# Half of each row normalisation moved from VectorE to ScalarE, with the result stored from the normalised rows' tile and a newly written step order

## The chip, the cores and the metric

The kernel runs on one core of a Trainium2 chip. The metric is device time in microseconds (us): from the start to the end of one execution. Five engines run their own instruction queues beside each other: TensorE (PE, matmuls and transposes; PEld is its loading of stationary operands), VectorE (DVE), ScalarE (ACT), GpSimd (POOL) and SyncE (SP, which issues nearly all DMAs here). An engine works through its queue strictly in the order in which the program writes it, and a semaphore wait at its head holds everything behind it.

## The reference, cut to what matters

The input `x` has 128 batches of 64 tokens of width 128, all fp32. `cond` gives each batch a vector and `ctx` each batch 64 context tokens. Four layers are applied one after the other:

```python
def _ln(x):                       # in every layer, before each projection
    mu = jnp.mean(x, axis=-1, keepdims=True); var = jnp.var(x, axis=-1, keepdims=True)
    return (x - mu) * jax.lax.rsqrt(var + EPS)
# layer 0 and layer 2 (16 heads of width 8, MLP of width 512)
xm = _ln(x) * (1.0 + sc_sa) + sh_sa              # sc, sh, g from silu(cond) @ W
x  = x + g_sa * (self_attention(xm @ W_qkv) @ W_proj)
x  = x + cross_attention(_ln(x) @ W_q, context) @ W_proj
xm = _ln(x) * (1.0 + sc_ff) + sh_ff
x  = x + g_ff * (gelu(xm @ W1 + b1) @ W2 + b2)
# layer 1: modulated cross attention; layer 3: router over 3 experts, and a gate
x = x + g * (routed @ out_w + out_b)
```

A group of four batches needs eight layer norms of `x` on its way through the four layers.

## The kernel before, in words

Four batches (256 tokens) make a group, 32 groups in all. A group's rows lie in a tile of 128 partitions x 2 x 128: two row blocks, t=0 and t=1. Six streams, s=0 to 5, each with its own set of tiles, work on six groups at once; a stream takes group s, then s+6, and so on. A group is 91 steps (`GROUP_STEPS`): load, stats, normal, context, cols, q, k, v, tops, lows, scores, values, out, and so on to l3_out and store. Each step may put instructions on several engines.

**What sets the order.** `SEQUENCE` is a string of 2930 characters. A digit means "the next step of that stream", an `f` means "the next of the 18 set-up steps" (`FOLDS`: modulations, gates, products of weights). `interleave()` turns it into `ORDER`, and every engine writes its instructions by walking through `ORDER`. So the one string fixes the order on all engines. It consists of a head of 243 steps, a piece of 546 steps (six groups) that stands four times in a row, and an end of 503 steps. `HALVES` says for each of the 320 attention score sets which half of PSUM it takes.

**A layer norm** goes over four engines: `stats` (lines 1097 to 1104) lets VectorE take means and variances; POOL adds eps and takes the power -0.5 (lines 696, 698, tile `rstd`); `normal` (line 1109) lets VectorE compute `(x - mean) * rstd` for t=0 and t=1 into `n_rows`; `cols` (line 740) lets TensorE transpose `n_rows`, after which VectorE modulates it, or ScalarE moves it, into `nT`. Between two stream steps of one stream stand steps of the other streams. POOL also prepares `lifted`, the residual plus bias (lines 708 and 711), and waits there for `gates`.

**The end of a group** (lines 1218 to 1220 and 651 to 656): VectorE writes the result over `x_rows`; SP stores `x_rows`, waits until the store has landed, and only then loads the next group into `x_rows`.

**The start.** SP issues conditions, small tables, the whole 1 MB of modulation weights, then rows and contexts of streams 0, 2 and 1 between further weights (lines 601 to 611). It waits for the gates' rows, stores them, waits, loads gates of four streams, and after that issues the other pieces of weights (line 598). TensorE's first `turn` step (line 786) waits for all the weights.

The code that the change touches, and what calls it:

## Time and profile before

| | |
|---|---|
| three timed runs | 1860.48, 1850.87, 1860.58 us; median 1860.48 |
| the profiled execution, its own time | 1857.61 us |
| its span, first to last instruction | 1855.6 us |
| around the span | 2.0 us |
| TensorE's granted clock over the span | 0.996 |
| PE busy, matmul instructions | 1758.5 us, 38181 |
| DVE busy | 1638.5 us |
| ACT busy | 1382.8 us |
| POOL busy | 643.6 us |

The profile names an instruction by its line in the kernel, its engine and the tiles it writes and reads (`out<-in`, buffer numbers left out, and `half` is PSUM). Each fp32 matmul shows as two records. Busy time of an engine is the union of its instructions' durations. "Idle before" is the engine's gap before an instruction, and the releaser is the instruction, on another engine, whose end let it go; "issue" is a gap that the profile puts down to nothing. A window's busy time over its length shows how close an engine is to filling it.

### The profile page before, as it was taken

What the parts mean: (1) busy time and instruction counts of PE and PEld (TensorE: products, weight loads), DVE (VectorE), ACT (ScalarE), POOL (GpSimd) and SP (SyncE); (2) the same over time, 40 slices, a digit from 0 to 9 for tenths busy, and PEclk for the clock granted to TensorE, in tenths of its full rate; (3) what the DMA queues carried; (4) which work ended last, traced back from release to release, by engine and by line L of the source; (5) the groups of instructions that cost most, each with busy time, mean ns of one, the idle gap of its engine ahead of it and who ended that gap; (6) DMA issues with size and microseconds to landing.
All of it is one profiled execution on the core that took longest, in us unless ns stands there. A gap on an engine that the chain in (4) does not pass through costs nothing.

```text
span 1855.6 us, 88109 instructions
## 1 busy us (share of the span) xinstructions
PE 1758.5 (95%) x38181; PEld 1505.4 (81%) x38181; DVE 1638.5 (88%) x4238; ACT 1382.8 (75%) x3341; POOL 643.6 (35%) x1145
## 2 busy tenths in 40 slices
PE   5988999999999999999999999999999999999898
PEld 4767788888788888888888888888888788887788
DVE  5889889999899999998999999899999989998874
ACT  2655777787787877777887787787777777777696
POOL 4222333343342343333233334233333333432341
PEclk9999999999999999999999999999999999999999
DMA  6000000001000000000000000000000000000000
GB/s 220 3 20 4 17 23 23 9 17 29 17 23 23 18 12 20 23 23 23 23 9 18 23 23 23 23 11 15 23 23 23 23 14 17 20 13 7 8 6 15
DMA packets 57693, 42.09 MB, mean 23 GB/s; under 512 B 13536, under 2 KB 56160, under 8 KB 57056
## 3 DMA queue, kind: packets, MB, share of 16 engines
q1 hardware_dynamic: 57312, 36.46, 6.7%
q8 instruction: 306, 5.01, 1.1%
q14 instruction: 75, 0.61, 0.1%
HBM read 31.99 MB, written 4.46 MB: 20 GB/s over the span
## 4 chain that ended last, share of the span: by engine, by line
PE 75%; DVE 13%; ACT 6%; issue 4%; DMA 0%; SPq 0%; POOL 0%; DVEq 0%; POOLq 0%
PE half L990 9%; PE half L888 8%; PE half L866 8%; PE half L892 7%; PE half L907 7%; PE half L935 5%; PE half L925 5%; DVE top L1136 4%; PE half L999 4%; PE half L740 4%; PE half L853 4%; PE half L918 3%; PE half L842 3%; PE half L838 3%; ACT pT L1335 2%
## 5 line engine op out<-in xcount | busy, mean ns | idle before, releaser
L1300 ACT ACTIVATE pT<-half 128x512 f32<-128x512 f32 x640 | 328.0, 610 | 103.2 <-PE half L892 102.2
L696 POOL TENSOR_TENSOR shifted<-moments,eps 128x2 f32<-128x2 f32 x256 | 50.6, 198 | 1010.7 <-DVE moments L1103 1010.7
L1136 DVE TENSOR_REDUCE top<-half 128x32 f32<-128x2048 f32 x160 | 365.0, 2281 | 30.7 <-PE half L866 29.3
L888 PE MATMUL half<-o_rows,of_keys 32*128 32x128 f32 x5120 | 274.4, 281 | 6.2 <-ACT o_rows L1229 2.9
L892 PE MATMUL half<-q_heads,k_heads 32*128 32x128 f32 x5120 | 262.2, 270 | 1.4 <-issue 1.3
L1335 ACT ACTIVATE pT<-half,mod 128x64 f32<-128x64 f32 x896 | 196.2, 332 | 54.3 <-PE half L990 53.2
L888 PEld LDWEIGHTS half<-o_rows,of_keys 32*128 32x128 f32 x5120 | 207.1, 186 | 29.1 <-issue 14.6
L892 PEld LDWEIGHTS half<-q_heads,k_heads 32*128 32x128 f32 x5120 | 209.1, 187 | 1.9 <-issue 1.9
L1276 ACT ACTIVATE k_heads<-half,key_bias,own_head_sb 128x256 f32<-128x256 f32 x320 | 163.4, 571 | 51.0 <-PE half L842 49.5
L866 PE MATMUL half<-k_heads,q_heads 32*128 32x128 f32 x5120 | 189.0, 281 | 9.6 <-issue 5.2
L1109 DVE TENSOR_SCALAR n_rows<-x_rows,moments,rstd 128x128 f32<-128x128 f32 x512 | 188.9, 415 | 6.8 <-POOL rstd L698 6.0
L698 POOL TENSOR_TENSOR rstd<-shifted,minus_halves 128x2 f32<-128x2 f32 x256 | 185.2, 723 | 20.1
L866 PEld LDWEIGHTS half<-k_heads,q_heads 32*128 32x128 f32 x5120 | 160.6, 186 | 37.4 <-issue 21.3
L907 PE MATMUL half<-pT,v_cols 128*32 128x64 f32 x10240 | 177.8, 221 | 10.3 <-issue 5.1
L907 PEld LDWEIGHTS half<-pT,v_cols 128*32 128x32 f32 x10240 | 153.7, 110 | 41.1 <-issue 32.4
L1128 DVE TENSOR_SCALAR q_heads<-half,b_sb,own_head_sb 128x256 f32<-128x256 f32 x320 | 156.5, 532 | 12.3 <-PE half L838 11.8
L1284 ACT ACTIVATE v_cols<-half 64x256 f32<-64x256 f32 x320 | 122.6, 383 | 24.6 <-PE half L853 22.4
L990 PE MATMUL half<-nT,w_sb 128*128 128x256 f32 x448 | 138.1, 390 | 0.1
L925 PE MATMUL half<-nT,w_sb 128*128 128x256 f32 x512 | 135.9, 394 | 1.0 <-DVE nT L1116 0.5
L1141 DVE STREAM_TRANSPOSE q_heads<-half 128x512 f32<-128x512 f32 x160 | 113.3, 708 | 26.3 <-PE half L907 23.6
L1305 ACT ACTIVATE pT<-half,b_sb 128x256 f32<-128x256 f32 x256 | 106.0, 471 | 38.5 <-PE half L925 37.3
L990 PE MATMUL half<-pT,w_sb 128*128 128x256 f32 x448 | 133.9, 380 | 0.6 <-issue 0.6
(148 smaller groups left out, 3755.2 us busy)
## 6 DMA issues: line engine op xcount, KB each, us to landing
gates<-gate_store SPq DMA_DIRECT2D x128, 128.0 KB, 3.1
x_rows<-x SPq DMA_DIRECT2D x32, 128.0 KB, 2.3
c_rows<-context SPq DMA_DIRECT2D x32, 128.0 KB, 2.4
out<-x_rows SPq DMA_DIRECT2D x32, 128.0 KB, 1.8
w_sb<-weights SPq DMA_DIRECT2D x1, 1856.0 KB, 10.5
pT<-weights SPq DMA_DIRECT2D x1, 1024.0 KB, 5.1
w_sb<-weights SPq DMA_DIRECT2D x2, 512.0 KB, 5.2
logit_bias<-logit_store SPq DMA_DIRECT2D x64, 1.5 KB, 3.5
```

Source lines behind the costliest of these rows:

```text
L698: nc.gpsimd.tensor_tensor(rstd[s][:, :], shifted[s][:, :], minus_halves[:, 0, :], ALU.pow).then_inc(rstd_in[s], 1)
L866: mm = nc.tensor.matmul(halves[HALF_OF[n]][:, g, tb * D:(tb + 1) * D], q_heads[s][part, tb, :, :], k_heads[s][part, tb, :, :], start=True, ...
L888: nc.tensor.matmul(halves[HALF_OF[n]][:, g, tb * D:(tb + 1) * D], of_keys[part, 2 * tb:2 * tb + 2, :], low[s][part, :], start=True, stop=F ...
L892: mm = nc.tensor.matmul(halves[HALF_OF[n]][:, g, tb * D:(tb + 1) * D], k_heads[s][part, tb, :, :], q_heads[s][part, tb, :, :], start=False ...
L907: mm = nc.tensor.matmul(dst[QUAD * g:QUAD * (g + 1), tb, :, lo, :], v_cols[s][:, at:at + QUAD], pT[s][:, g, tb, lo, :].rearrange("p (h q) ...
L925: mm = nc.tensor.matmul(dst[:, c * TOK:(c + 1) * TOK], w(layer["w1"], 0, 2 * half + c), nT[s][:, :, :], start=True, stop=True)
L990: mm = nc.tensor.matmul(dst[:, r * TOK:(r + 1) * TOK], weight, src[:, :, :], start=c == 0, stop=c == 1)
L1109: m = nc.vector.tensor_scalar(n_rows[s][:, t, :], x_rows[s][:, t, :], moments[s][:, t, 0:1], rstd[s][:, t:t + 1], ALU.subtract, ALU.mult)
L1136: nc.vector.tensor_reduce(top[s][:, :].rearrange("p (g c) -> p g c", c=32)[:, :, 0:2 * GROUP], halves[HALF_OF[n]][:, :, :].rearrange("p g ...
L1276: m = nc.scalar.activation(k_heads[s][:, :, pair, :], bank4(src), ACT.Identity, scale=own_head[:, pair:pair + 1], bias=key_bias[:, n_att, ...
L1300: nc.scalar.activation(turn_cols[s][:, g, :], halves[HALF_OF[n]][:, g, :], ACT.Exp, scale=ATT_SCALE).then_inc(scores_read, 1)
L1335: m = nc.scalar.activation(dst, src[:, at], ACT.Silu, bias=mod[s][:, k, tb:tb + 1])
```

## The change

1. **normal.** VectorE normalises only t=0. POOL computes one more value, `minus = -mean * rstd` for t=1 (128x1), and ScalarE normalises t=1 as `Identity(rstd * x + minus)`. TensorE's transposes wait for both (`rows_normed` counts to 2).
2. **End of a group.** VectorE writes the result into `added`, which is the same tile as `n_rows`. SP stores from there and issues the next group's `x` at once. The wait for the store moves to VectorE, before the next group's `stats` (and for all streams to SP's end).
3. **Start.** Of the modulation weights the 768 columns of layer 0 come first; the other 1280 columns follow after layer 0's own weights, with a semaphore of their own (`later_mods_in`) that `gates` waits for. All remaining weights and the fourth stream's rows are issued ahead of the wait for the gates' rows. The copy of the first modulations to a stream moves from `load` to the first `cols`.
4. **Order.** `SEQUENCE` and `HALVES` are new strings, of the same lengths (2930 and 320), again a head of 243 steps, 546 steps four times, and an end of 503. Tiles that set-up borrows from streams now go by the order in which streams start or score.

```diff
-    "ff02410210002300f202f0222f110f320313f203201f0100f301132f010410f31024203f202111f310023f1014f2041f3001"
+    "f023101200f0f11100f02104312f10102f31303120f23021f00023f04312f01420f11201f40310f32300f22104f22031f020"
...
-                load_weights(W_LOADS[0], 0, W_LOADS[0][3], mod_weights_in)
-                load_rows(0)
+                load_weights(W_LOADS[0], 0, MOD_L0_COLS, mod_weights_in)
+                load_rows(BY_START[0])
                 load_weights(W_LOADS[1], 0, L0_COLS, l0_weights_in)
-                load_rows(2)
+                load_weights(W_LOADS[0], MOD_L0_COLS, W_LOADS[0][3] - MOD_L0_COLS, later_mods_in)
+                load_rows(BY_START[1])
...
                 load_weights(W_LOADS[1], L0_COLS, W_LOADS[1][3] - L0_COLS, weights_in)
+                for load in W_LOADS[2:]:
+                    load_weights(load, 0, load[3], weights_in)
+                load_rows(BY_START[3])
 
                 sp.wait_ge(v_emptied, used_by(FOLD_AT["gates", None], FOR_VECTOR))
                 sp.dma_start(gate_store, gate_rows[0:B, :]).then_inc(gates_stored, 16)
-                load_rows(3)
                 sp.wait_ge(gates_stored, 16)
...
-                        sp.dma_start(rows_of(out, s, r), x_rows[s][:, :, :]).then_inc(stored[s], 16)
-                        sp.wait_ge(stored[s], 16 * (r + 1))
+                        sp.dma_start(rows_of(out, s, r), added[s][:, :, :]).then_inc(stored[s], 16)
                         if r + 1 < ROUNDS[s]:
                             sp.dma_start(x_rows[s][:, :, :], rows_of(x, s, r + 1)).then_inc(x_in[s], 16)
...
+                        count.next(rstd_in[s])
+                        nc.gpsimd.tensor_scalar(minus[s][:, :], moments[s][:, 1, 0:1], -1.0, rstd[s][:, 1:2], ALU.mult, ALU.mult).then_inc(minus_in[s], 1)
...
                     if kind == "cols":
-                        count.next(rows_normed[s])
+                        count.next(rows_normed[s], 2)
...
                     if kind == "gates":
+                        pe.wait_ge(later_mods_in, 16)
...
                     if kind == "stats":
                         dve.wait_ge(*x_changed(n))
+                        if residual_before(n)[0] is None and round_of(n):
+                            dve.wait_ge(stored[s], 16 * round_of(n))
...
                     if kind == "normal":
                         count.next(rstd_in[s])
-                        for t in range(2):
-                            m = nc.vector.tensor_scalar(n_rows[s][:, t, :], x_rows[s][:, t, :], moments[s][:, t, 0:1], rstd[s][:, t:t + 1],
-                                                        ALU.subtract, ALU.mult)
-                        m.then_inc(rows_normed[s], 1)
+                        nc.vector.tensor_scalar(n_rows[s][:, 0, :], x_rows[s][:, 0, :], moments[s][:, 0, 0:1], rstd[s][:, 0:1],
+                                                ALU.subtract, ALU.mult).then_inc(rows_normed[s], 1)
...
-                        nc.vector.scalar_tensor_tensor(out=x_rows[s][:, :, :], in0=added[s][:, :, :], scalar=0.5, in1=x_rows[s][:, :, :],
+                        nc.vector.scalar_tensor_tensor(out=added[s][:, :, :], in0=added[s][:, :, :], scalar=0.5, in1=x_rows[s][:, :, :],
                                                        op0=ALU.mult, op1=ALU.add).then_inc(x_added[s], 1)
...
+                    if kind == "normal":
+                        count.next(minus_in[s])
+                        nc.scalar.activation(n_rows[s][:, 1, :], x_rows[s][:, 1, :], ACT.Identity, scale=rstd[s][:, 1:2],
+                                             bias=minus[s][:, :]).then_inc(rows_normed[s], 1)
```

What the new order makes of the engines' queues is shown at three places. First TensorE in the start, before, from the end of the first exp scores on. `half0<-ident_sb,w_sb` (L786) is the first `turn` step, `top2` the second stream's maxima, and `o_rows2,of_keys` begins the second stream's scores:

```order
L740 MATMUL half0<-ident_sb,n_rows1 128x128 x2
L740 MATMUL half0<-ident_sb,c_rows3 128x128 x2
L786 MATMUL half0<-ident_sb,w_sb 128x128
L786 MATMUL half0<-ident_sb,pT4 128x128 x2
L786 MATMUL half0<-ident_sb,w_sb 128x128
L877 MATMUL half0<-ident_sb,top2 128x128
L907 MATMUL half0<-pT0,v_cols0 32x2x32 x32
L740 MATMUL half0<-ident_sb,n_rows3 128x128 x2
L888 MATMUL half1<-o_rows2,of_keys 128x128 x4
```

The same place now; the second stream to start is stream 1, and L753, L775, L800, L891, L902 and L921 are the former L740, L762, L786, L877, L888 and L907:

```order
L753 MATMUL half0<-ident_sb,n_rows2 128x128 x2
L775 MATMUL half0<-pT4,pT5 128x128 x4
L891 MATMUL half0<-ident_sb,top1 128x128
L753 MATMUL half0<-ident_sb,c_rows3 128x128 x2
L921 MATMUL half0<-pT0,v_cols0 32x2x32 x32
L753 MATMUL half0<-ident_sb,n_rows3 128x128 x2
L902 MATMUL half1<-o_rows1,of_keys 128x128 x4
```

The `turn` step that waits for all weights has moved from before the first values (`pT0,v_cols0`) and the second scores to behind them.

Second, VectorE at its first instructions of the loop, before: modulations, their copies and the statistics of three streams.

```order
L1050 TENSOR_SCALAR mods<-half,b_sb 128x128 x4
L1029 COPY mod<-mods 128x16 x4
L1100 BN_STATS stats<-x_rows 128x6 x2
L1103 BN_AGGR moments<-stats 128x2 x2
L1100 BN_STATS stats<-x_rows 128x6 x2
L1103 BN_AGGR moments<-stats 128x2 x2
L1100 BN_STATS stats<-x_rows 128x6 x2
L1103 BN_AGGR moments<-stats 128x2 x2
L1109 TENSOR_SCALAR n_rows<-x_rows,moments,rstd 128x128 x2
```

And now:

```order
L1113 BN_STATS stats<-x_rows 128x6 x2
L1116 BN_AGGR moments<-stats 128x2 x2
L1113 BN_STATS stats<-x_rows 128x6 x2
L1116 BN_AGGR moments<-stats 128x2 x2
L1113 BN_STATS stats<-x_rows 128x6 x2
L1116 BN_AGGR moments<-stats 128x2 x2
L1121 TENSOR_SCALAR n_rows<-x_rows,moments,rstd 128x128
L1103 BN_STATS c_stats<-c_rows 128x6 x2
L1105 BN_AGGR c_moments<-c_stats 128x2 x2
L1064 TENSOR_SCALAR mods<-half,b_sb 128x128 x4
L1043 COPY mod<-mods 128x16
```

The statistics of three streams still stand ahead of the first normalisation; the modulations have moved behind it.

Third, ScalarE's queue in the repeated piece, as it is now (before, its queue held no `n_rows`). L1319 is the exp of the scores, L1295, L1303 and L1243 move keys, values and other tiles out of PSUM:

```order
L1319 ACT_TABLE_LOAD
L1319 ACTIVATE pT1<-half1 128x512 x4
L1360 ACTIVATE kvT3<-kvT3 128x256
L1295 ACTIVATE k_heads5<-half0,key_bias,own_head_sb 128x4x64 x2
L1303 ACTIVATE v_cols5<-half0 64x32x8 x2
L1279 ACTIVATE n_rows5<-x_rows5,minus5,rstd5 128x128
L1279 ACTIVATE n_rows4<-x_rows4,minus4,rstd4 128x128
L1295 ACTIVATE k_heads2<-half0,key_bias,own_head_sb 128x4x64 x2
```

The normalisation of t=1 stands between moves out of PSUM, and whatever follows it on ScalarE waits if POOL's `minus` is late.

## Rows read from the trace of the kernel before

**Rows 1.** The page: busy times of the engines, and the chain that ended last, by engine.

```profile
PE 1758.5 (95%) x38181; PEld 1505.4 (81%) x38181; DVE 1638.5 (88%) x4238; ACT 1382.8 (75%) x3341; POOL 643.6 (35%) x1145
...
PE 75%; DVE 13%; ACT 6%; issue 4%; DMA 0%; SPq 0%; POOL 0%; DVEq 0%; POOLq 0%
```

**Rows 2.** Windows: length, then busy us (instructions) of each engine; granted clock; DMA share; GB/s.

```profile
0.00:165.00 165.00, 127.23 (x2852) 106.17 (x2856) 125.67 (x320) 76.61 (x175) 48.94 (x108) 0.97 0.22 69
165.00:1492.00 1327.00, 1290.45 (x28394) 1105.59 (x28390) 1208.60 (x3136) 1031.63 (x2475) 478.47 (x842) 1.00 0.07 20
655.32:986.02 330.70, 324.21 (x7141) 278.15 (x7141) 304.09 (x788) 260.50 (x625) 119.95 (x211) 1.00 0.07 20
1492.00:1800.00 308.00, 290.85 (x6541) 247.92 (x6536) 276.14 (x691) 233.00 (x540) 102.39 (x176) 1.00 0.04 12
```

**Rows 3.** Chain that ended last, whole span, 200 longest pieces: start, us, what.

```profile
324.06 3.65 PE half L990 x16
...
1318.91 3.65 PE half L990 x16
```

**Rows 4.** Waits of PE in one period: releaser, us in total, times, longest.

```profile
PE half L740 <- ACT pT L1335: 1.2, 1, 1.2
PE half L877 <- DVE n_rows L1022: 0.8, 1, 0.8
PE half L907 <- issue: 0.7, 1, 0.7
...
PE half L877 <- DVE top L1136: 0.3, 1, 0.3
```

**Rows 5.** Chain that ended last, 0 to 60 us: start, us, what.

```profile
7.02 6.76 DMA x_rows<-x
...
33.53 6.91 issue
...
44.22 0.46 PE half L888 x8
```

**Rows 6.** Timeline of SP's DMA issues, 0 to 60 us: start, us, what.

```profile
21.30 0.34 SPq L615 DMA_DIRECT2D gate_store<-pT  x1
...
23.38 5.99 SPq L582 DMA_DIRECT2D gates<-gate_store  x8
...
35.04 0.43 SPq L598 DMA_DIRECT2D pT<-weights  x1
```

**Rows 7.** Timeline of PE, 0 to 60 us: start, us, what, idle before.

```profile
41.67 1.94 PE L907 MATMUL half<-pT,v_cols 128*32 128x64 f32 x64
...
53.10 1.10 PE L907 MATMUL half<-pT,v_cols 128*32 128x64 f32 x64
```

**Rows 8.** Timeline of DVE, 0 to 60 us.

```profile
9.94 1.13 DVE L1050 TENSOR_SCALAR mods<-half,b_sb 128x128 f32<-128x128 f32 x4 [3.44 <-PE half L762]
...
14.49 0.57 DVE L1109 TENSOR_SCALAR n_rows<-x_rows,moments,rstd 128x128 f32<-128x128 f32 x2
```

**Rows 9.** Timeline of POOL, 0 to 75 us.

```profile
28.19 0.73 POOL L708 TENSOR_TENSOR lifted<-gates,row_sb 128x256 f32<-128x256 f32 x1 [10.27 <-DMA gates<-gate_store]
```

**Rows 10.** Groups of instructions by shape: count, busy us, mean ns, idle before.

```profile
L1109 DVE TENSOR_SCALAR n_rows<-x_rows,moments,rstd 128x128 f32<-128x128 f32 x512 | 188.9, 415 | 6.8 <-POOL rstd L698 6.0
...
L1259 ACT ACTIVATE nT<-c_rows,c_minus,c_rstd 128x128 f32<-128x128 f32 x128 | 56.2, 496 | 0.1
...
L693 POOL TENSOR_SCALAR c_minus<-c_minus 128x4 f32<-128x4 f32 x32 | 7.4, 232 | 2.9
```

**Rows 11.** Who waited for the normalised rows (L1109): us, times.

```profile
  PEld half L740: 14.1, 14
```

**Rows 12.** SP's transfers of x_rows, who waited for one, and the page's store and load.

```profile
  DVE stats L1100: 0.5, 1
...
x_rows<-x SPq DMA_DIRECT2D x32, 128.0 KB, 2.3
out<-x_rows SPq DMA_DIRECT2D x32, 128.0 KB, 1.8
```

More of the change, by code:

```diff
@@ L215 @@
-    "0000011110001110001111111111100000000111110000001111110000011111100001111011111111110000110000110000"
-    "00001000001001111100"
+    "0011110011110011111100110011000011100011111111111000001110000011111110000011111100001111100011100011"
+    "1111111110000011100000111111100000111111000011111000111000111111111110000011100000111111100000111111"
+    "0000111110001110001111111111100000111000001111111000001111110000111110001001110000111110000011111001"
+    "11110000110011111111"
 )
@@ L273, in first_scores @@
     return min(n for n, (kind, _, t) in enumerate(ORDER) if kind == "scores" and t == s)
+BY_SCORES = sorted(range(STREAMS), key=first_scores)
+BY_START = sorted(range(STREAMS), key=lambda s: min(n for n, (kind, _, t) in enumerate(ORDER) if kind == "stats" and t == s))
+assert max(FOLD_AT.values()) < first_scores(BY_SCORES[4])
 def next_step(n):
@@ L426, in build @@
         shifted, rstd = each("shifted", [D, 2]), each("rstd", [D, 2])
+        minus = each("minus", [D, 1])
         c_shifted, c_rstd, c_minus = each("c_shifted", [D, 2, 2]), each("c_rstd", [D, 2, 2]), each("c_minus", [D, 2, 2])
@@ L470, in build @@
         routed = n_rows
-        early = {MOD_ONLY: turn_cols[5].rearrange("p n c -> p (n c)"), SET_UP_ONLY: turn_cols[4].rearrange("p n c -> p (n c)")}
-        turned = turn_cols[5][:, 0:3, :].rearrange("p n (m c) -> p (n m) c", c=D)
-        gate_rows, gate_bias = turn_cols[3][:, 3, :], gates[5][:, :, :, :].rearrange("p t n c -> p (t n) c")
-        cond_rows, cond_silu, logit_rows = turn_cols[4][0:B, 3, 0:D], turn_cols[4][:, 3, D:D + B], turn_cols[4][:, 3, 2 * D:2 * D + EXPERTS]
+        early = {MOD_ONLY: turn_cols[BY_SCORES[5]].rearrange("p n c -> p (n c)"), SET_UP_ONLY: turn_cols[BY_SCORES[4]].rearrange("p n c -> p (n c)")}
+        turned = turn_cols[BY_SCORES[5]][:, 0:3, :].rearrange("p n (m c) -> p (n m) c", c=D)
+        gate_rows, gate_bias = turn_cols[BY_SCORES[3]][:, 3, :], gates[BY_START[5]][:, :, :, :].rearrange("p t n c -> p (t n) c")
+        spare = turn_cols[BY_SCORES[4]][:, 3, :]
+        cond_rows, cond_silu, logit_rows = spare[0:B, 0:D], spare[:, D:D + B], spare[:, 2 * D:2 * D + EXPERTS]
         logit_store = nc.dram_tensor("logit_store", (B, EXPERTS), F32, kind="Internal").ap()
@@ L482, in build @@
         small_in = first_sem
-        mod_weights_in, l0_weights_in, weights_in, rows_in, gate_bias_in = (sem(name) for name in (
-            "mod_weights_in", "l0_weights_in", "weights_in", "rows_in", "gate_bias_in"))
+        mod_weights_in, later_mods_in, l0_weights_in, weights_in, rows_in, gate_bias_in = (sem(name) for name in (
+            "mod_weights_in", "later_mods_in", "l0_weights_in", "weights_in", "rows_in", "gate_bias_in"))
         consts_made, key_bias_made = sem("consts_made"), sem("key_bias_made")
@@ L504, in build @@
         o_turned = sem("o_turned")
+        minus_in = [sem(f"minus_in{s}") for s in range(STREAMS)]
         p3_done, p3_normed = [sem(f"p3_done{s}") for s in range(STREAMS)], [sem(f"p3_normed{s}") for s in range(STREAMS)]
@@ L652, in _ @@
                         sp.wait_ge(*x_changed(n))
-                        sp.dma_start(rows_of(out, s, r), x_rows[s][:, :, :]).then_inc(stored[s], 16)
-                        sp.wait_ge(stored[s], 16 * (r + 1))
+                        sp.dma_start(rows_of(out, s, r), added[s][:, :, :]).then_inc(stored[s], 16)
                         if r + 1 < ROUNDS[s]:
                             sp.dma_start(x_rows[s][:, :, :], rows_of(x, s, r + 1)).then_inc(x_in[s], 16)
+                for s in range(STREAMS):
+                    sp.wait_ge(stored[s], 16 * ROUNDS[s])
             @block.gpsimd
```

79 lines of the change are left out of this document (38 added, 41 removed).

## The prediction

> **What bounds the kernel now.** I read the page's busy times and its chain first. TensorE is busy for 1758.5 of 1855.6 us (95%), VectorE for 88%, ScalarE for 75%, and three quarters of the chain that ended last are TensorE's [rows 1]. So TensorE is the bound, and the change removes no matmul: all that can be won is its idle time, 1855.6 - 1758.5 = 97 us, and what the order lets it do faster. A table by windows shows where those 97 us lie [rows 2]. I cut it at the repetitions of the step order, which show in the trace as a period: the same long block of L990 stands at 324.06 us and, three repetitions later, at 1318.91 us, so 331.6 us each [rows 3]. Until 165 us TensorE is idle for 165.0 - 127.2 = 38 us. In the repeated part, 165 to 1492 us, it is idle for 1327.0 - 1290.5 = 36.5 us, 2.8%, and in one period for 330.7 - 324.2 = 6.5 us. From 1492 to 1800 us it is idle for 17 us, while VectorE is busy for 276 of 308 us (90%). In the last 56 us it is idle for 6 us, in a drain that the change leaves alone.
>
> Then I read who ends the idle time. In the second of those periods VectorE ended five waits of TensorE worth 2.0 us (0.8 us the longest, 0.3 us the last), ScalarE four worth 2.1 us (1.2 us the longest), and "issue" three worth 1.6 us [rows 4]. No wait stands out, and VectorE ended about a third. In the start one does: 6.91 us from 33.53 us on, in the chain, put down to "issue" [rows 5]. It is TensorE at the first `turn` step. The profile names no releaser, but the step waits for all weights, and the last of them were issued at 35.04 us, because SP had waited for the gates' rows (stored at 21.30 us) and then issued eight gate loads (23.38 to 29.37 us) ahead of them [rows 6].
>
> **The change part by part.** I make the sum against the profiled execution: 1857.6 us, 2.0 us more than its span. The median of the three runs is 1860.5 us, 2.9 us above it; the number at the end is on the median's scale.
>
> *The start.* All weights are now issued ahead of the wait for the gates' rows, and the `turn` step stands behind the first values and the second scores. The 6.9 us go. Of two equal blocks of values, the one behind the gap took 1.94 us and the next 1.10 us [rows 7], so another 0.8 us goes with it. The first window's granted clock is 0.97 and the later ones' 1.00 [rows 2]. The page "TensorE: Matmul & The Clock Gate" of the Trainium skill, part 1, says that an idle TensorE falls from 2.4 to 1.2 GHz and needs sustained work to come back. By that rule a gap of this length costs more than itself, which the two blocks agree with; without the rule the term would be 6.9 us alone.
>
> Against this stand two delays. VectorE still takes three streams' statistics before its first normalisation, and the third stream's x landed at 7.02 + 6.76 = 13.78 us [rows 5]. The queue ahead of it holds the same bytes in another order (768 + 1280 columns for 2048), so splitting the modulation weights wins nothing there. But the modulations (four instructions, 1.13 us [rows 8]) now stand between that normalisation and its modulation: +1 us. And the gate rows' store now queues behind twelve more weight loads and a stream's rows, some 2.3 MB. Before, the weights took from 29.4 us, when SP began to issue them, until TensorE's release at 40.4 us: 11 us. Now their issue begins some 12 us before the store's 21.3 us. I take the store as 0 to 5 us late. POOL stood waiting for these gates until 28.19 us [rows 9], and now `lifted` of two streams and then the fourth stream's `rstd` stand behind that wait. Late by 5 us, it would release them at 33 us, and the second stream's scores would follow some 4 us later. Before, they began at 44.22 us [rows 5], so this is covered up to about 7 us. Start: -6.9 - 0.8 + 1.0 = -6.7, say -7 us; bounds -11 (the second scores come as early as the queues allow) and +3 (the gates take all of it).
>
> *Half the normalisation.* VectorE loses 256 of 512 instructions of 188.9/512 = 0.37 us busy each: 94 us. ScalarE gains 256. The nearest row is its normalisation of the context, same shape and source, 56.2/128 = 0.44 us each [rows 10]: 113 us. POOL gains 256 instructions near `c_minus` at 0.23 us: 59 us. By period, with 48 of them, VectorE goes from 304 to 286 us, ScalarE from 260 to 282 us, POOL from 120 to 131 us, all against TensorE's 324 [rows 2]. No engine overtakes TensorE. The Trainium skill's "ScalarE: Activation LUTs", under its rules for kernel authors, says adds and multiplies belong on VectorE, not ScalarE. The rows agree in price, 0.44 against 0.37 us, and by the rule the work of both grows by 18 us. It would decide only if ScalarE were full; that is the third rival.
>
> VectorE with 6% less to do hands its results over earlier. I take the third of TensorE's idle time that VectorE ends: 36.5/3 = 12 us in the repeated part and 17/3 = 6 us between 1492 and 1800 us, of which I take 5, since the end's order must also empty six streams. Bounds: nothing, if TensorE's other releasers are just behind, and all of the 36.5 and 17 us.
>
> *The longer path of a norm.* Before: `rstd`, then VectorE's pair, 0.57 us where nothing disturbs it [rows 8]. Now: `rstd`, 0.23 us on POOL, then 0.50 us (the mean) on ScalarE [rows 10]: +0.16 us, which I round up to 0.24 us for the gap between two dependent instructions on POOL, a choice of mine. That is 256 x 0.24 = 61 us if nothing covered it. TensorE's weight loads waited for normalised rows 14 times [rows 11]; only there is it uncovered: 14 x 0.24 = 3 us. Bounds 3 and 30 us (half uncovered). Behind a late `minus` on ScalarE stand moves of keys and values out of PSUM, and TensorE waits for those.
>
> *Store and load.* SP no longer holds 26 times for a store of 1.8 us before it loads x (2.3 us). VectorE waited 0.5 us for x in the whole trace, once [rows 12], so the gain is 0. The new wait on VectorE, for a store issued ahead of that load and landing sooner, is 0 too; if it were late, statistics and everything behind them on VectorE would wait. The later copy of the modulations is the same instruction in another place: 0.
>
> Sum: 1857.6 - 7 - 12 - 5 + 3 = 1836.6 us, and 2.9 us more on the median's scale: 1839.5, so 1840 us.
>
> **The rivals.**
>
> 1. *Only the start.* TensorE's waits in the repeated part are short and spread over three kinds of releaser [rows 4]. If taking VectorE out of a wait only uncovers ScalarE's, now busier, the period stays at 331 us. For it: no wait of over 1.2 us in a period. Against it: the chain runs through VectorE for 13% and ScalarE for 6% [rows 1]. Then -7 and -2 at the end: 1851.5, so 1852 us.
> 2. *The new order is better than VectorE's relief alone.* With the order rewritten the idle time in the repeated part could halve and the end lose 10 us: -10 - 18 - 10 + 3 = -35, so 1826 us. For it: some of the 324 us busy per period may be blocks stretched by late operands. Against: the piece repeated has the same 546 steps.
> 3. *ScalarE becomes the late engine: slower.* Its queue holds blocks of four exps and table loads. A t=1 half that falls behind one is late for TensorE's transposes, where VectorE's pair was in time, and a late `minus` holds moves out of PSUM. If half of the 256 norms expose 0.24 us, that is 31 us; less the start's 7 and a few of VectorE's relief it gives 1860.5 + 31 - 13 = 1878 us. It decides once ScalarE's queue runs more than about 0.3 us behind on most norms, and would show as a period above 335 us. Against it: ScalarE at 282 of 331 us keeps 15% of slack.
> 4. *The start does not do what it says.* The gate rows' store waits so long behind the weights that POOL's wait passes 35 us and TensorE stands idle for as long as before. With rival 1 that is 1859 us.
>
> **How the numbers follow.** Forecast, 1840 us: 0.47, own range 1828 to 1852. Rival 1, 1852 us: 0.26. Rival 2, 1826 us: 0.13. Rival 3, 1878 us: 0.10. Rival 4, 1859 us: 0.04. A change under about 0.5%, 9 us, can't be told from none here. Faster than 1851: 0.45 of the forecast, all of rival 2 and a third of rival 1, 0.66. Within 0.5%: the rest of these, and rival 4, 0.24. Slower than 1870: rival 3, 0.10. The range reaches from 1822, 4 us under rival 2, to 1862, past rivals 1 and 4, and leaves out rival 3 and a tail of rival 2.
>
> **What would show it.** Start: no gap of TensorE over 3 us between 30 and 45 us, the second scores at 33 to 38 us, POOL's wait for gates ending between 28 and 33 us. Repeated part: a period of 328 to 330 us, VectorE near 286 and ScalarE near 282 us in it, and less idle time before TensorE ended by VectorE. Norms: the ScalarE normalisation near 0.44 us busy each, POOL's `minus` near 0.23 us. End: less than 14 us idle of TensorE in the 300 us before the last 56. The prediction is wrong in its middle term if the period stays at 331 us, and wrong in sign if it exceeds 335 us with ScalarE as TensorE's main releaser.

## The result and the profile after

The changed kernel took 1833.6 us in the median of four runs (1830.3 to 1836.0), the kernel before 1860.0 us in four runs beside it (1850.9 to 1860.6): a ratio of 0.9877, 95% interval 0.9855 to 0.9898, 1.2% faster (the two medians alone, divided, give 0.986). I had forecast 1840 us, range 1822 to 1862. The profiled execution took 1832.7 us with a span of 1830.8 us, 24.8 us less than the span before; the sum had promised 21.

Busy times of the engines and the chain that ended last, of the changed kernel's page (against [rows 1]):

```profile
PE 1751.3 (96%) x38181; PEld 1503.1 (82%) x38181; DVE 1554.5 (85%) x3982; ACT 1484.3 (81%) x3598; POOL 717.2 (39%) x1401
...
PE 83%; DVE 8%; ACT 5%; issue 3%; DMA 1%; SPq 1%; DVEq 0%
```

VectorE lost 84 us, ScalarE gained 102, POOL 74. TensorE's own busy time fell by 7 us, and it now holds 83% of the chain instead of 75%. The same long block of `projected` matmuls, L1004 now, in the chain that ended last (start, us, what):

```profile
471.51 3.46 PE half L1004 x16
798.03 3.46 PE half L1004 x16
1128.62 3.46 PE half L1004 x16
1457.32 3.46 PE half L1004 x16
```

That is (1457.32 - 471.51) / 3 = 328.6 us a period, 3.0 less than the 331.6 of [rows 3]; four periods give 12 us. One by one they take 326.5, 330.6 and 328.7 us, against 331.3, 330.7 and 332.9 before. The windows, with the columns of [rows 2]; the second line is the longest of the three periods:

```profile
190.00:1500.00 1310.00, 1282.65 (x28420) 1104.88 (x28418) 1145.74 (x2934) 1119.50 (x2685) 528.91 (x1024) 1.00 0.07 20
798.03:1128.62 330.59, 323.25 (x7141) 278.29 (x7141) 288.07 (x739) 281.82 (x676) 133.50 (x258) 1.00 0.07 20
1500.00:1775.00 275.00, 262.57 (x5899) 222.54 (x5898) 234.59 (x590) 217.35 (x532) 108.44 (x209) 1.00 0.04 13
```

In a period VectorE is busy for 288 us (forecast 286) and ScalarE for 282 (forecast 282). All three periods in one window, first of the kernel before and then of the changed one:

```profile
324.06:1318.91 994.85, 972.97 (x21422) 834.51 (x21421) 910.36 (x2358) 781.48 (x1875) 358.37 (x631) 1.00 0.07 20
```

```profile
471.51:1457.32 985.81, 967.65 (x21422) 833.14 (x21421) 865.59 (x2221) 846.38 (x2027) 401.19 (x777) 1.00 0.08 20
```

For the same 21422 matmul records TensorE is busy 5.3 us less, and it is idle for 18.2 us instead of 21.9. So of the 3.0 us that a period lost, 1.8 are matmuls that took less time and only 1.2 are idle time. In these windows the view of waits gives VectorE 6.6 us of TensorE's idle time before (18 waits) and 4.6 now (8), ScalarE 6.6 (16) and 2.5 (8), and "issue" 6.7 (9) and 9.2 (15).

In the 275 us before the last 56, TensorE is idle for 12.4 us. The kernel before, cut the same way (1525 to 1800 us), was idle for 17.1:

```profile
1525.00:1800.00 275.00, 257.85 (x5870) 218.77 (x5869) 246.98 (x617) 206.28 (x479) 92.47 (x159) 1.00 0.05 14
```

The start on TensorE: the first normalised rows, the first scores, the first values, the second stream's scores and the first `turn` step (L800) of the changed kernel (start, us, what, idle before; against [rows 5, 7]):

```profile
15.98 0.69 PE L753 MATMUL half<-ident_sb,n_rows 128*128 128x128 f32 x2 [6.70 <-DVE n_rows L1121]
...
30.59 0.50 PE L902 MATMUL half<-o_rows,of_keys 32*128 32x128 f32 x8 [1.11 <-DVE mods L1064]
...
34.86 1.10 PE L921 MATMUL half<-pT,v_cols 128*32 128x64 f32 x64 [0.44 <-ACT pT L1319]
36.26 0.50 PE L902 MATMUL half<-o_rows,of_keys 32*128 32x128 f32 x8
...
39.23 0.27 PE L800 MATMUL half<-ident_sb,w_sb 128*128 128x128 f32 x1
```

No gap before the `turn` step, and the second scores begin at 36.3 instead of 44.2 us, 8 us earlier. The first block of values takes 1.10 us, where the one behind the gap took 1.94 [rows 7]. The window behind the gap, in the kernel before, shows a granted clock of 0.50:

```profile
40.44:43.70 3.26, 3.26 (x70) 2.76 (x71) 0.03 (x1) 0.77 (x2) 1.10 (x2) 0.50 0.59 139
```

In the changed kernel it is 1.00 in the block of values and in the second scores. POOL still waits for the gates, until 30.8 us (against [rows 9]):

```profile
30.78 0.73 POOL L721 TENSOR_TENSOR lifted<-gates,row_sb 128x256 f32<-128x256 f32 x1 [8.23 <-DMA gates<-gate_store]
```

And the three instructions of the split, by shape (count, busy us, mean ns, idle before; against [rows 10]):

```profile
L1279 ACT ACTIVATE n_rows<-x_rows,minus,rstd 128x128 f32<-128x128 f32 x256 | 127.4, 504 | 29.6 <-POOL minus L711 27.6
...
L1121 DVE TENSOR_SCALAR n_rows<-x_rows,moments,rstd 128x128 f32<-128x128 f32 x256 | 98.2, 390 | 12.3 <-POOL rstd L709 11.8
L711 POOL TENSOR_SCALAR minus<-moments,rstd 128x1 f32<-128x1 f32 x256 | 73.7, 288 | 26.2
```

By the group's row ScalarE's half costs 0.50 us of busy time, not 0.44, and POOL's `minus` 0.29, not 0.23.

So the start, the length of a period, the busy times in it and the end showed what I had forecast; where a period's 3.0 us come from did not. And that the places agree doesn't show that the parts of the change earn what I gave them, and the experiments say that they don't.

### The profile page after: what moved, and what is told of

Its sections match the earlier page's. It is cut to its first block, busy times and chain, and to the rows that moved or that the text cites. A ratio compares the mean times of both kernels' runs of the same rounds, so it can differ in the third digit from the quotient of the medians.

```text
span 1830.8 us, 88396 instructions
## 1 busy us (share of the span) xinstructions
PE 1751.3 (96%) x38181; PEld 1503.1 (82%) x38181; DVE 1554.5 (85%) x3982; ACT 1484.3 (81%) x3598; POOL 717.2 (39%) x1401
## 4 chain that ended last, share of the span: by engine, by line
PE 83%; DVE 8%; ACT 5%; issue 3%; DMA 1%; SPq 1%; DVEq 0%
PE half L1004 10%; PE half L902 8%; PE half L880 8%; PE half L921 8%; PE half L906 7%; PE half L939 6%; PE half L949 6%; PE half L1013 4%; PE half L753 4%; PE half L932 4%; PE half L867 4%; PE half L852 4%; PE half L856 3%; DVE top L1150 3%; ACT pT L1319 1%
## 5 line engine op out<-in xcount | busy, mean ns | idle before, releaser
L1319 ACT ACTIVATE pT<-half 128x512 f32<-128x512 f32 x640 | 330.0, 607 | 76.0 <-PE half L906 74.9
L902 PE MATMUL half<-o_rows,of_keys 32*128 32x128 f32 x5120 | 277.2, 282 | 7.8 <-issue 4.8
L902 PEld LDWEIGHTS half<-o_rows,of_keys 32*128 32x128 f32 x5120 | 208.5, 186 | 31.1 <-issue 18.7
L921 PE MATMUL half<-pT,v_cols 128*32 128x64 f32 x10240 | 177.7, 220 | 9.2 <-ACT pT L1319 4.6
L921 PEld LDWEIGHTS half<-pT,v_cols 128*32 128x32 f32 x10240 | 153.3, 110 | 38.7 <-issue 31.9
L1295 ACT ACTIVATE k_heads<-half,key_bias,own_head_sb 128x256 f32<-128x256 f32 x320 | 164.3, 573 | 24.3 <-PE half L856 22.7
L1279 ACT ACTIVATE n_rows<-x_rows,minus,rstd 128x128 f32<-128x128 f32 x256 | 127.4, 504 | 29.6 <-POOL minus L711 27.6
L1113 DVE BATCH_NORM_STATS2 stats<-x_rows 128x6 f32<-128x128 f32 x512 | 122.4, 281 | 21.5 <-DMA x_rows<-x 18.4
L1303 ACT ACTIVATE v_cols<-half 64x256 f32<-64x256 f32 x320 | 122.7, 383 | 20.6 <-PE half L867 17.6
L1004 PE MATMUL half<-nT,w_sb 128*128 128x256 f32 x448 | 137.1, 387 | 2.1 <-issue 2.1
L1004 PE MATMUL half<-pT,w_sb 128*128 128x256 f32 x448 | 133.2, 379 | 0.7 <-issue 0.7
L949 PE MATMUL half<-w_sb,pT 128*128 128x128 f32 x1024 | 127.5, 277 | 1.0 <-DVE top L1150 0.6
```

The source lines that it names most:

```text
L902: nc.tensor.matmul(halves[HALF_OF[n]][:, g, tb * D:(tb + 1) * D], of_keys[part, 2 * tb:2 * tb + 2, :], low[s][part, :], start=True, stop=F ...
L921: mm = nc.tensor.matmul(dst[QUAD * g:QUAD * (g + 1), tb, :, lo, :], v_cols[s][:, at:at + QUAD], pT[s][:, g, tb, lo, :].rearrange("p (h q) ...
L949: mm = nc.tensor.matmul(dst[:, t * D:(t + 1) * D], hidden[s][:, c, t * D:(t + 1) * D], w(arg["w2"], c), start=c == 0, stop=c == 3)
L1004: mm = nc.tensor.matmul(dst[:, r * TOK:(r + 1) * TOK], weight, src[:, :, :], start=c == 0, stop=c == 1)
L1295: m = nc.scalar.activation(k_heads[s][:, :, pair, :], bank4(src), ACT.Identity, scale=own_head[:, pair:pair + 1], bias=key_bias[:, n_att, ...
L1319: nc.scalar.activation(turn_cols[s][:, g, :], halves[HALF_OF[n]][:, g, :], ACT.Exp, scale=ATT_SCALE).then_inc(scores_read, 1)
```

## The experiments

Each ratio is against the kernel before, on the same chip, with a 95% interval; the kernel before had medians of 1856.6, 1852.4 and 1855.8 us in the three sets. Edits are against the changed kernel unless the text says "before".

### The split and the order, apart

**e1: the new order, both halves on VectorE.**

```diff
-                        count.next(rows_normed[s], 2)
+                        count.next(rows_normed[s])
...
-                        nc.vector.tensor_scalar(n_rows[s][:, 0, :], ...).then_inc(rows_normed[s], 1)
+                        for t in range(2):
+                            m = nc.vector.tensor_scalar(n_rows[s][:, t, :], ..., ALU.subtract, ALU.mult)
+                        m.then_inc(rows_normed[s], 1)
...
-                        nc.gpsimd.tensor_scalar(minus[s][:, :], ...)
-                        nc.scalar.activation(n_rows[s][:, 1, :], ...)
```

> The changed kernel with VectorE normalising both halves again, in the new order; POOL's minus and ScalarE's half are gone. Theory (VectorE's relief carries the repeated part and the end, 17 us of the 26 gained): 1848 to 1855 us, the period back to 331 us or more, VectorE near 304 us busy in it. Rival (the new order does it, whoever normalises): 1830 to 1838 us.

1.0006 (0.9993 to 1.0018): nothing. The new order, the new start and the new store, all three together but without the split, are worth nothing. Waits of TensorE in this kernel (releaser, us in total, times, longest):

```profile
PE half L751 <- DVE n_rows L1120: 18.1, 22, 6.9
```

The same line of the changed kernel:

```profile
PE half L753 <- DVE n_rows L1121: 9.5, 5, 6.7
PE half L753 <- ACT n_rows L1279: 1.7, 4, 0.8
```

With both halves on VectorE, TensorE waits for normalised rows 22 times instead of 9. The start's gain is there in e1 too (second scores at 35.3 us), and the repeated part gives it back: its block of L1011 returns after 335.2 and then 332.6 us.

The matmuls of e1 and of the changed kernel stand in the same order, so the two can be laid side by side. The block near the end of the repeated part and the one just before the drain, first in e1 and then in the changed kernel (chain that ended last; start, us, what):

```profile
1477.02 3.46 PE half L1002 x16
1800.74 3.46 PE half L1002 x16
```

```profile
1457.32 3.46 PE half L1004 x16
1774.60 3.46 PE half L1004 x16
```

e1 is 19.7 us behind at the first and 26.1 at the second, and 26.2 at the end of the span. In this order the split is worth 19.7 us up to the first block and 6.4 us from there to the second.

**e3: before, with the split alone, in the old order.** The edit is e1's, the other way round, on the kernel before.

```diff
+                        count.next(rstd_in[s])
+                        nc.gpsimd.tensor_scalar(minus[s][:, :], moments[s][:, 1, 0:1], -1.0, rstd[s][:, 1:2], ALU.mult, ALU.mult)...
...
-                        count.next(rows_normed[s])
+                        count.next(rows_normed[s], 2)
...
+                    if kind == "normal":
+                        count.next(minus_in[s])
+                        nc.scalar.activation(n_rows[s][:, 1, :], x_rows[s][:, 1, :], ACT.Identity, ...)
```

> The kernel before with only the normalisation split between VectorE and ScalarE, old order, old start, old end of a group. Theory: 12 us in the repeated part and 5 at the end, less 3 for the longer path: 1843 to 1850 us. Rival (ScalarE late in an order not made for it): 1860 to 1880 us.

1.0635 (1.0612 to 1.0657): 116 us slower. Busy times in the page of e3:

```profile
PE 1792.0 (91%) x38181; PEld 1522.8 (77%) x38181; DVE 1560.9 (79%) x3982; ACT 1486.8 (76%) x3597; POOL 714.2 (36%) x1401
```

VectorE's and ScalarE's work are those of the changed kernel within 7 us; neither is full (79 and 76%). The waits of TensorE, and of ScalarE, in e3:

```profile
PE half L744 <- ACT n_rows L1267: 55.8, 49, 3.1
PE half L744 <- DVE n_rows L1112: 5.0, 3, 4.7
...
ACT n_rows L1267 <- POOL minus L702: 63.5, 36, 8.2
```

One of the 49 in e3's chain that ended last (start, us, what):

```profile
700.43 1.28 ACT L1307
701.72 0.01 issue
701.73 4.03 ACT pT L1307 x8
705.75 0.37 ACT n_rows L1267
706.12 0.04 issue
706.16 0.44 PE half L744 x2
```

ScalarE's half stands behind a table load and eight exps, and the transposes come 3.14 us late. POOL's `minus` for this half had long been there (timelines of POOL and of PE):

```profile
696.42 0.27 POOL L702 TENSOR_SCALAR minus<-moments,rstd 128x1 f32<-128x1 f32 x1
```

```profile
706.16 0.44 PE L744 MATMUL half<-ident_sb,n_rows 128*128 128x128 f32 x2 [3.14 <-ACT n_rows L1267]
```

So it is in all 49 waits of the trace: `minus` was ready at least 1.2 us, in the median 4.3 us, before TensorE had come to the transposes, and the half itself takes 0.50. In 25 of them the instruction just ahead of the half on ScalarE is an exp, in 23 a move of values. A late `minus` counts only indirectly: in 6 of the 49 the unbroken row of ScalarE's work ahead of the half had begun when a `minus` arrived. Of the 110 us by which e3's span is longer, 76 are idle time of TensorE and 34 longer matmuls.

**e2: the changed kernel with the old order.** `SEQUENCE` and `HALVES` are the old strings, all else is new.

> The changed kernel's code with the strings of the order of before. Theory (relief and start work in any order, since ScalarE has room): 1838 to 1848 us. Rival (the order is what gains; ScalarE's half stands where nobody planned it): 1853 to 1865 us.

1.063 (1.0601 to 1.0659), the same as e3: both my expectations were wrong. Together e1 to e3 and the change itself make a table:

| | both halves on VectorE | t=1 on ScalarE |
|---|---|---|
| old order | 1 | 1.0635 (e3), 1.063 (e2, with the new start and store) |
| new order | 1.0006 (e1) | 0.9877 (the change) |

The parts don't add. The split costs 6.3% in the old order and wins 1.3% in the new one.

**e13: before with the split, and ScalarE's half still further back.** ScalarE's half is issued at the `cols` step instead of the `normal` step, behind what ScalarE does between the two.

```diff
-                    if kind == "normal":
+                    if kind == "cols":
                         count.next(minus_in[s])
                         nc.scalar.activation(n_rows[s][:, 1, :], ...)
```

> The kernel before with the split alone, and ScalarE's half written at the cols step instead of the normal step, so that minus is surely there and ScalarE holds nothing up, but the half starts later. If ScalarE's loss in the old order is its waiting for minus (63.5 us) with other work queued behind: ratio 1.00 to 1.03 instead of 1.06. If it is that the half comes too late for TensorE (55.8 us in 49 waits): 1.06 or more, with longer waits of TensorE for n_rows.

1.2427 (1.2387 to 1.2468). Waits in e13, and then its busy times:

```profile
PE half L744 <- ACT n_rows L1267: 345.9, 208, 3.4
...
ACT n_rows L1267 <- POOL minus L702: 3.5, 1, 3.5
```

```profile
PE 1895.0 (82%) x38181; PEld 1591.1 (69%) x38181; DVE 1562.9 (68%) x3982; ACT 1496.9 (65%) x3597; POOL 711.5 (31%) x1401
```

Between e3 and e13 only the half's place in ScalarE's queue differs, and the late norms go from 49 to 208; in the new order they are 4. ScalarE's wait for `minus` is gone in e13 (3.5 us), and it is the slowest of all. By itself that doesn't clear `minus` in e3, since the edit also makes the half later; the 49 waits above do. What makes the half late is its place in ScalarE's queue, against that of the transposes in TensorE's.

### The start

**e5: the changed kernel with the old SP order.**

```diff
-                load_weights(W_LOADS[0], 0, MOD_L0_COLS, mod_weights_in)
+                load_weights(W_LOADS[0], 0, W_LOADS[0][3], mod_weights_in)
...
-                for load in W_LOADS[2:]:
-                    load_weights(load, 0, load[3], weights_in)
...
                 sp.wait_ge(gates_stored, 16)
...
+                for load in W_LOADS[2:]:
+                    load_weights(load, 0, load[3], weights_in)
```

> The changed kernel with SP's start as before: modulation weights in one load, the other weights issued behind the gate loads. Theory (the turn step now stands behind the second scores, so the order alone hides most of the 6.9 us, but the weights land only near 40 us): 1833 to 1838 us, 0 to 4 us slower than the changed kernel. Rival (SP's order is what removed the gap): 1839 to 1843 us.

0.9878 (0.9865 to 0.9892), the ratio of the change itself. TensorE shows no gap at the `turn` step and the second scores begin at 35.4 us. The start's gain comes from the string, which puts that step behind the second scores; SP's order adds nothing to it. What it costs is late gates. In e5 POOL has the gates at 24.1 us:

```profile
24.11 0.73 POOL L720 TENSOR_TENSOR lifted<-gates,row_sb 128x256 f32<-128x256 f32 x1 [2.77 <-DMA gates<-gate_store]
```

In the changed kernel it has them 6.7 us later. There the gate rows' store was issued at 19.69 us and the gates' loads, which SP issues when it has landed, at 26.73; in e5 at 18.30 and 20.35. Those 6.7 us make no difference in time that can be told.

**e6: before, with only the weights and the fourth stream's rows ahead of the gates' wait.**

```diff
+                for load in W_LOADS[2:]:
+                    load_weights(load, 0, load[3], weights_in)
+                load_rows(3)
...
                 sp.wait_ge(gates_stored, 16)
...
-                for load in W_LOADS[2:]:
-                    load_weights(load, 0, load[3], weights_in)
```

> The kernel before with one edit: all weights and the fourth stream's rows issued ahead of the wait for the gates' rows. Theory (the gap at the turn step goes, the gates come a few us later): 6 to 8 us faster than before, 1849 to 1851 us. Rival (the later gates, which POOL waits for, take it back): within 2 us of before, 1855 to 1859 us.

0.998 (0.9968 to 0.9993), 3.7 us. The 6.9 us at the `turn` step are gone, but another wait stands just behind. TensorE's timeline in e6, the first values and the second scores:

```profile
38.30 1.79 PE L907 MATMUL half<-pT,v_cols 128*32 128x64 f32 x64 [3.83 <-DVE nT L1116]
...
40.65 0.81 PE L888 MATMUL half<-o_rows,of_keys 32*128 32x128 f32 x8
```

The chain that ended last names it (start, us, what):

```profile
25.98 2.88 DMA gates<-gate_store
...
29.03 0.74 POOL lifted L708
...
36.04 0.73 POOL rstd L698
36.77 0.03 issue
36.80 0.60 DVE n_rows L1109 x2
37.40 0.35 DVE half L1115
...
37.77 0.43 DVE nT L1116
```

POOL waits for the gates, does 7 us of other work that had queued behind them, then the `rstd` on which TensorE's next tile depends. Over half of the removed gap is given back there. The 3.7 us lie between my two expectations.

**e10: the changed kernel, with the first stream's statistics and normalisation ahead of the others'.** One line of `SEQUENCE`:

```diff
-    "f023101200f0f11100f02104312f..."
+    "f0231000f01f111200f02104312f..."
```

> The changed kernel, and in the first steps the first stream's statistics and normalisation come first, the second's statistics behind its modulation, the third's after that; TensorE's order is unchanged. In the changed kernel TensorE waited 6.7 us for the first normalised rows, until 15.98 us. Theory (the start is kept by the stream that waits): the first transposes at 9 to 10 us and 3 to 6 us off the time, ratio to before 0.984 to 0.986. Rival (the gate rows, which POOL waits for until 30.8 us, are the bound of the start): the ratio stays at 0.987 to 0.989.

0.9864 (0.9846 to 0.9882). The first normalised rows reach TensorE at 9.6 instead of 16.0 us, yet it then waits 4.22 us before the first scores for the modulations, and 1.36 us for ScalarE's half of normalised rows just ahead of the second stream's scores, which begin at 37.2 us. The interval holds the change's ratio: no difference that can be told.

**e11: e10, with the gates' rows stored ahead of the last weights and the fourth stream's rows.**

> The kernel of e10_stats_later, and SP issues the gate rows' store and then the last weights and the fourth stream's rows, before it waits for the store. Theory of the gates: POOL's wait ends by 27 us instead of 30.8, the second scores begin by 32 us, and another 2 to 4 us go: ratio 0.981 to 0.985. Rival: no more than e10_stats_later.

0.9868 (0.9854 to 0.9881). The store is issued at 14.3 instead of the 20.2 us of e10 and the gates' loads from 21.6 instead of 27.1 us on, but POOL has them only at 30.7 us, as before the edit (30.9 in e10). I had expected them earlier; the moved issue didn't bring the data sooner. The second scores begin at 36.2 us, behind a wait of 4.62 us for ScalarE's half. What the gates wait for, the weights in flight or something else, wasn't separated.

### The size of the smaller terms

**e4: store from `x_rows`, SP waits, then loads, as before the change.**

```diff
-                        sp.dma_start(rows_of(out, s, r), added[s][:, :, :]).then_inc(stored[s], 16)
+                        sp.dma_start(rows_of(out, s, r), x_rows[s][:, :, :]).then_inc(stored[s], 16)
+                        sp.wait_ge(stored[s], 16 * (r + 1))
```

> The changed kernel with the result written over x again, stored, waited for, and only then x loaded. Theory as predicted (early load worth nothing): 1831 to 1836 us. Rival (the new order puts the next group's statistics so close behind its load that VectorE waits 18 us for x already; 2 us more in each of 26 loads then cost TensorE some): 1840 to 1855 us.

0.9902 (0.9884 to 0.9921), 0.0025 or some 5 us more than the change, with intervals that overlap. VectorE waited for x for 23.0 us in e4. Who waited for a load of `x_rows`, in the changed kernel (against [rows 12]):

```profile
  DVE stats L1113: 18.4, 8
```

The old order left 0.5 us of such waits, this one 18.4, in which the early load can be worth something.

**e8: VectorE computes t=1 too, into a spare tile that nobody reads.** It waits for its own result.

```diff
+                        own_result(nc.vector.tensor_scalar(spare_rows[:, :], x_rows[s][:, 1, :], moments[s][:, 1, 0:1], rstd[s][:, 1:2],
+                                                           ALU.subtract, ALU.mult))
```

> The changed kernel, and VectorE normalises t=1 as well, right behind t=0, into a spare tile that nobody reads: VectorE's load is that of before, ScalarE's that of after, and the row's path is not longer. Theory (what VectorE does less of is what gains): 1850 to 1858 us, as with VectorE doing both halves. Rival (two engines in parallel make one norm shorter, the load does not matter): 1832 to 1838 us.

1.0104 (1.0087 to 1.0121): 42 us slower than the change for 91 us more VectorE work (1645.4 against 1554.5 us). That is 0.46 us for each us, and it contains the wait for the own result, which the real pair in e1 didn't have. (e1 itself, which also takes the half off ScalarE, is 24 us slower than the change for 79 us more of VectorE's work.) I had expected 1850 to 1858 us if VectorE's load is what gains, and 1832 to 1838 if it is that two engines work on one norm at once. The second is refuted: here both still do, and the gain is gone. The first was too small, by some 14 us.

**e9: POOL computes `minus` twice, one behind the other.**

```diff
+                        nc.gpsimd.tensor_scalar(minus[s][:, :], ...).then_inc(pool_own, 1)
+                        count.next(pool_own)
                         nc.gpsimd.tensor_scalar(minus[s][:, :], ...).then_inc(minus_in[s], 1)
```

> The changed kernel with POOL computing minus twice, the second after the first: ScalarE's half can start some 0.34 us later in each of 256 norms, 87 us in all if nothing covered it. Theory as predicted (14 uncovered places): +3 to +6 us, 1836 to 1840 us. Rival (ScalarE waits in its queue and holds keys and values behind it, as in the old order): +20 us or more, 1853 us and above.

0.9937 (0.9916 to 0.9958): 11 us slower than the change, between the 3 to 6 us of my theory and the 20 and more of its rival. POOL is busy 68.5 us longer, 0.27 us a norm, 0.34 with the gap between two dependent instructions (0.07 us in the chains). So 256 norms, 87 us later in all, cost 11 us, or 0.13 us per us. TensorE waited for ScalarE's half 7 times instead of 4, for 3.1 instead of 1.7 us; most of the 11 us doesn't show in the waits for that tile.

**e14: the group's last step on POOL** instead of VectorE (the product by 0.5 and the sum with x, two instructions of POOL for one of VectorE and its wait for its own result).

```diff
-                        nc.vector.scalar_tensor_tensor(out=added[s][:, :, :], in0=added[s][:, :, :], scalar=0.5, in1=x_rows[s][:, :, :], ...)
+                        nc.gpsimd.tensor_scalar(added[s][:, :, :], added[s][:, :, :], 0.5, None, ALU.mult)...
+                        nc.gpsimd.tensor_tensor(added[s][:, :, :], added[s][:, :, :], x_rows[s][:, :, :], ALU.add)...
```

> The changed kernel with the last step of a group on POOL: VectorE makes (gate + 1) * routed, POOL halves it and adds x, and VectorE loses 32 instructions of 0.53 us and a wait on its own result each, 18 us. Theory (VectorE's work counts at 0.4 us per us, from the run with its load put back): 4 to 8 us faster than the changed kernel, ratio 0.983 to 0.986. Rival (POOL waits at the head of its queue for VectorE's result while statistics of other streams stand behind it): slower than the changed kernel, ratio 0.990 to 1.000.

0.9874 (0.986 to 0.9889), the change's ratio again, with VectorE at 1539.2 us and POOL at 768.0. Taking 15 us off VectorE here, at the price of 51 us more on POOL, wins nothing, though e8 priced VectorE's time at 0.46 us per us. Either VectorE's time is worth less at this place than at the normalisation, or the longer way over POOL takes the gain back; the run doesn't separate the two. e8's price can't be carried to another place as it stands.

## Why the prediction was right in size and wrong in its reasons

*TensorE is the bound; its idle time is what can be won.* Right. Its idle time fell from 97 to 79.5 us and its busy time by 7 us, together the 24.8 us.

*The start, -7 us.* Right in size: the second scores come 8 us earlier, and the block behind the former gap is 0.8 us shorter. That block was not the whole price of the clock: TensorE worked for 3.26 us at a granted clock of 0.50 behind the gap, where half, some 1.6 us, is an estimate of what a full clock would have saved. Right that the `turn` step's new place removes the gap, but the half of the change to which I gave equal credit, the weights issued early, is worth nothing beside it (e5) and 3.7 us without it (e6). In e6 it is POOL's wait for the gates that takes over, the mechanism that I had named under the start and covered "up to about 7 us". That cover was the string's doing too: against e5 the gates come 6.7 us later, and the time is the same. My "0 to 5 us late" looked at the issue of the store, which moved by 1.4 us; what grew was its way to landing, from about 2 to 7 us.

*The repeated part, -12 us.* Right in number, by luck of the rule. I took the third of TensorE's idle time that VectorE ended. In the three periods that part fell by 2.0 us, which makes some 3 in four, not 12; the rest of the period's gain is shorter matmuls (1.8 us of 3.0) and fewer waits for ScalarE, which I had not counted. The step that failed is the assumption behind it: that the split can be priced on the old order's waits. By e3, on those very waits, it costs 116 us. And the 12 us are a difference of two larger things: without the split the new order's period is longer than the old one (335.2 and 332.6 us in e1, 331.6 before), and the split takes 19.7 us off by the block at 1457 us.

*The end, -5 us.* The last 275 us before the drain lost 4.7 us of idle time. e1 tells what earned it: without the split, in the same order, the way from the last period's block to the one before the drain takes 6.4 us more.

*The longer path, +3 us.* Too small. I counted the 14 places at which TensorE waited for normalised rows [rows 11]. e9 priced a further 0.34 us per norm at 11 us. At that slope the delay that I had assumed, 0.24 us a norm, is some 8 us, an extrapolation from one point. A delay off TensorE's direct waits still shifts work behind it on ScalarE and VectorE.

*Store and load, 0.* Close: the early load may be worth about 5 us (e4, not clear of the interval), since this order leans on it. Before the change, VectorE's 0.5 us of waiting [rows 12] was a property of the old order, not of the kernel.

*ScalarE's half at 0.44 us.* It had to serve for two things and is right for neither. For how long one half takes it is too small, because I took a busy time per instruction from a group whose instructions run in pairs [rows 10]; the busy time is a union, and what overlaps in a pair is counted once. The row's own mean, 496 ns, was the figure to use; now it is 504. For what 256 of them add to the engine it is too large: ScalarE's busy time is 98.8 us above that of e1, 0.39 us for each, since a half also overlaps neighbours of other lines. VectorE in the same way gave back 79.4 us, 0.31 for each and not 0.37. The Trainium skill ("ScalarE: Activation LUTs", under "What ACT_TABLE_LOAD costs") gives 186 ns + 0.833 ns an element and some 93 ns for each pointer operand, with an overlap of some 93 ns back to back. An estimate by it is 479 ns for this one and 386 ns beside a neighbour; the fastest in the trace agree with the first (477 ns), and the 0.39 us with the second.

*Rival 3, ScalarE late.* Its mechanism is the strongest effect in this study and I gave it the wrong lever and, with 31 us where e3 lost 116, a quarter of its size. I reasoned from ScalarE's slack ("15%") and a latency of 0.24 us, and got +18 us. What decides is where the order puts the half on ScalarE against its use on TensorE: 49 late norms of 1.1 us each in the old order, with ScalarE at 76%. I knew that the string had changed and had its rows in front of me; I should have counted, at each of the 256 norms, what stands between on both queues, instead of arguing from the load. The Trainium skill ("Perfetto Trace Analysis", under "Optimizing Scalar/DVE Operations") says that with a saturated VectorE, offloading work to ScalarE may make sense. Both signs are measured here, with VectorE at 88%: +6.3% and -1.3% for the same offload.

*Rival 1, only the start*, is refuted by the period; *rival 2*, a better order by itself, by e1, though its remark that some busy time may be blocks stretched by late operands fits the 1.8 us a period. *Rival 4*, the gates later than 35 us, is refuted by POOL's 30.8.

What stays open: how much of e8's 42 us is load and how much its wait for its own result; through which waits the split gains in the new order, since those for normalised rows (18.1 us in e1, 11.2 in the changed kernel) are a small part of it; why e14 wins nothing; and what holds the gates' data in e11. No experiment kernel beats the changed one measurably: e10 has the lowest ratio, 0.9864, with an interval that holds 0.9877.

## What to carry to other kernels

When work moves to another engine, price its place in that engine's in-order queue against the place of its first consumer, use by use, before its duration or the engine's busy share: the same 256 instructions made this kernel 1.3% faster, 6.3% slower or 24% slower. A change that comes as an edit with a new order has no price for the edit and price for the order; measure the two apart only to learn which needs which. And behind a gap that is to go, look for the next wait by its dependency chain (here the gates on POOL), since that sets what the gap is worth.

## What the runs showed of the hardware

- ScalarE's `Identity` with pointers for scale and bias took 0.49 us in the median for 128x128 in fp32 from SBUF to SBUF, where VectorE's `(x - a) * b` took 0.34 us.
- TensorE's granted clock over the whole span was 0.997 in the changed kernel, 0.983 in e3 and 0.937 in e13, where it was busy for 82% in many short waits. Its busy time for the same 38181 matmuls rose to 1792 and 1895 us, against 1758 before, so waits cost more than their own length. In e10 the scores right behind the wait of 4.22 us rose to 0.73 us a block, with a granted clock of 0.58 from 28.80 to 32.10 us; in the changed kernel the same scores take 0.43 us a block, at 1.00. Behind the gap of 6.91 us in the kernel before it was 0.50, the lower of the clock's two levels (1.2 and 2.4 GHz).
- A load of x issued right behind the same group's store took 2.8 us to land in the median, 2.3 us when SP had waited for the store [rows 12]. It isn't the order: the old order without that wait gave 2.7 us (e2), the new one with it 2.4 (e4).
